# The first expert loop of a MetaFormer block: single chunks through the gate, high halves before low halves, and weight scans issued from another queue

## The reference, cut to what matters

```python
t = _to_tokens(x)                                    # 4096 tokens of 256 values
h = jnp.einsum('nd,ehd->neh', xf, w1)                # xf = layernorm(t); w1, w3: 8 x 512 x 256
g = jnp.einsum('nd,ehd->neh', xf, w3)
eo = jnp.einsum('neh,edh->ned', jax.nn.silu(h) * g, w2)
out = jnp.einsum('ned,ne->nd', eo, comb)             # comb: weights of the two chosen experts
```

## Time and profile before

| | |
|---|---|
| median of 3 runs | 1333.01 us (1328.87 to 1334.24) |
| the profiled execution, its time | 1335.55 us |
| its span, first to last instruction | 1333.8 us |
| PE busy | 945.6 us, 71% |
| DVE busy | 873.4 us, 65% |
| ACT busy | 514.4 us, 39% |
| POOL busy | 442.6 us, 33% |
| mean granted clock of TensorE | 0.811 of full speed |

### The profile page before, as it was taken

How to read it: one execution, slowest core, us unless ns; L and a number is a source line. 1 busy time by engine, 2 the same in 40 slices (tenths; PEclk the granted TensorE clock), 3 DMA queues, 4 the chain that set the end, 5 groups by cost and what they waited for, 6 DMA issues and landing times.

```text
span 1333.8 us, 25140 instructions
## 1 busy us (share of the span) xinstructions
PE 945.6 (71%) x7185; PEld 794.4 (60%) x7185; DVE 873.4 (65%) x1854; ACT 514.4 (39%) x983; POOL 442.6 (33%) x486
## 2 busy tenths in 40 slices
PE   5210577656399999999800668457999999999943
PEld 4100456515288888888700457416888888888842
DVE  6999789897444555555589886683555555555545
ACT  5200223276354444444433443283443333443312
POOL 1285000000045555555522560003444434444410
PEclk8655795558799999999955885557999999999975
DMA  7000007806633555455567312104222232222257
GB/s 229 1 0 0 0 1 224 280 0 201 227 88 94 155 154 155 99 154 158 152 214 241 126 63 77 50 0 103 72 79 71 77 78 75 75 75 75 75 165 252
DMA packets 169438, 147.22 MB, mean 110 GB/s; under 512 B 88432, under 2 KB 152376, under 8 KB 169272
## 3 DMA queue, kind: packets, MB, share of 16 engines
q1 hardware_dynamic: 151048, 103.76, 27.0%
q0 software_dynamic: 14000, 38.82, 9.1%
q10 hardware_dynamic: 4352, 4.20, 1.0%
HBM read 96.39 MB, written 30.93 MB: 95 GB/s over the span
## 4 chain that ended last, share of the span: by engine, by line
PE 57%; DVE 21%; issue 8%; DMA 6%; ACT 5%; SPq 1%; DVEq 1%; ACTq 0%; POOLq 0%; POOL 0%
PE bank L711 27%; PE bank L729 18%; PE bank L647 4%; PE bank L564 3%; DVE tok L1373 2%; DMA wreg<-rows_y 2%; DVE region L1032 2%; PE bank L764 2%; ACT xt L869 2%; DVE xt L1044 2%; DMA wreg<-in_L_ffn_w_dram 1%; PE bank L619 1%; DVE region L1031 1%; DVE region L1343 1%; PE bank L689 1%
## 5 line engine op out<-in xcount | busy, mean ns | idle before, releaser
L711 PE MATMUL bank<-xt,wreg 128*128 x3360 | 382.5, 274 | 30.9 <-DMA xt<-region 30.9
L711 PEld LDWEIGHTS bank<-xt,wreg 128*128 128x128 f16 x3360 | 330.7, 98 | 71.4 <-issue 31.3
L729 PE MATMUL bank<-wreg,region 128*128 128x256 f16 x2520 | 292.6, 273 | 16.2 <-DVE region L1347 15.1
L729 PEld LDWEIGHTS bank<-wreg,region 128*128 128x128 f16 x2520 | 243.6, 98 | 54.0 <-DVE region L1347 24.6
L891 ACT ACTIVATE region<-bank,b_t,fac 128x256 f32<-128x256 f32 x280 | 142.5, 560 | 226.3 <-PE bank L711 215.7
L495 POOL DMA_INDIRECT rows_y<-region,put_now x140 | 138.4, 988 | 221.4 <-DVE region L1358 140.3
L455 POOL DMA_INDIRECT region<-rows_x,fetch_now x144 | 144.4, 1003 | 185.8 <-DMA xt<-region 94.0
L1343 DVE SCALAR_TENSOR_TENSOR region<-bank,fac,region 128x256 f32<-128x256 f32 x140 | 61.2, 479 | 157.8 <-PE bank L711 106.7
L564 PE MATMUL bank<-ident,xn 128*128 128x128 f32 x256 | 56.6, 383 | 112.6 <-DVE xn L1003 104.4
L1350 DVE TENSOR_SCALAR region<-region,fac 128x512 f16<-128x512 f32 x140 | 76.5, 546 | 69.3 <-ACT region L891 64.2
L564 PEld LDWEIGHTS bank<-ident,xn 128*128 128x128 f32 x256 | 45.8, 208 | 121.3 <-DVE xn L1003 110.6
(11 more groups left out here) (237 smaller groups left out, 1238.7 us busy)
## 6 DMA issues: line engine op xcount, KB each, us to landing
wreg<-in_L_ffn_w_dram SPq DMA_DIRECT2D x48, 512.0 KB, 5.9
wreg<-in_L_ffn_w_dram SPq DMA_DIRECT2D x16, 1024.0 KB
wreg<-rows_y SPq DMA_DIRECT2D x48, 256.0 KB, 3.6
region<-in_L_ffn_w_dram SPq DMA_DIRECT2D x12, 1024.0 KB, 7.4
rows_x<-region SPq DMA_DIRECT2D x16, 512.0 KB, 3.2
wreg<-in_x_dram SPq DMA_DIRECT2D x4, 1024.0 KB, 9.4
out_dram<-xt ACTq DMA_DIRECT2D x16, 256.0 KB, 3.6
xt<-region SPq DMA_TRANSPOSE x148
```

What stands on the lines that cost most here:

```text
L711: last = pe.matmul(to, w[:, e, k, ws_, c * P:(c + 1) * P], x_cols[:, bass.ds(b, 1), :, xs_, k, :].rearrange("p j r n -> p (j r) n"), start ...
L729: last = pe.matmul(yb[:, r * C:(r + 1) * C], lhs[:, c, r * P:(r + 1) * P], w[:, e, c, ws_, :], start=first, stop=end, skip_group_check=True)
```

## The change

It has three parts. In `up` of f = 0 PE takes one chunk at a time, `w1` into the left half of a bank and `w3` into the right half, and counts `z_ready` once a chunk; ACT's Silu and DVE's product then go chunk by chunk. In `down` PE does the four matmuls of a chunk that read the high half ahead of the two that read the low half, and for f = 0 it waits for each half apart. The scan loads are issued by ACT: one ahead of the loop, each later one behind an expert's tiles.

```diff
 SP
-            sp.wait_ge(w_lo[0], 6 * E)
-            for e in range(2):
-                load_scan(e)
...
-                    if f == 0 and 1 <= e < E - 1:
-                        sp.wait_ge(scanned, e)
-                        load_scan(e + 1)
 PE, up
-                ws = ((w1_s, zb[2 * (h % 2)]), (w3_s, zb[2 * (h % 2) + 1])) if f == 0 else ((v1_s, zb[h]),)
-                for w, z in ws:
-                    for c in (2 * h, 2 * h + 1):
-                        to = z[:, (c % 2) * TILE:(c % 2 + 1) * TILE]
+                ws = (w1_s, w3_s) if f == 0 else (v1_s,)
+                for c in (2 * h, 2 * h + 1):
+                    for m, w in enumerate(ws):
+                        z, at = (zb[c], m) if f == 0 else (zb[h], c % 2)
+                        to = z[:, at * TILE:(at + 1) * TILE]
...
-                    last.then_inc(z_ready[f], 1)
+                    if f == 0 or c % 2:
+                        last.then_inc(z_ready[f], 1)
 PE, down
-                        pe.wait_ge(lo_ready[0], 2 * halves * tile + c + 1)
+                        pe.wait_ge(hi_ready[0], 2 * halves * tile + c + 1)
...
-                    for r in range(2):
-                        for hs, ws_ in PARTS:
-                            lhs = (hid_hi, hid_lo)[hs]
+                    for hs in range(2):
+                        if f == 0 and hs == 1:
+                            pe.wait_ge(lo_ready[0], 2 * halves * tile + c + 1)
+                        lhs = (hid_hi, hid_lo)[hs]
+                        for r, ws_ in ((0, 0), (0, 1), (1, 0), (1, 1)) if hs == 0 else ((0, 0), (1, 0)):
 ACT
+            def load_scan(n):
+                e = E - 1 - n
+                act.dma_start(scan1[:, n % 2, 0].rearrange("p (c h) -> p c h", c=KC),
+                             v1[e].rearrange("(c p) h -> p c h", p=P)).then_inc(scan_loaded[n % 2], 16)
+                act.dma_start(scan1[:, n % 2, 1].rearrange("p (c d) -> p c d", c=8),
+                             v2[e].rearrange("(c p) d -> p c d", p=P)).then_inc(scan_loaded[n % 2], 16)
...
+                if f == 0:
+                    act.wait_ge(w_lo[0], 6 * E)
+                    load_scan(0)
...
-                                act.wait_ge(z_ready[0], 2 * halves * n + 2 * h + 1)
-                                act.activation(gate_act[:, h], zb[2 * h][:], ACT.Silu, scale=fac[:, 0, e:e + 1]
-                                               ).then_inc(silu_done[f], 1)
+                                for c in (2 * h, 2 * h + 1):
+                                    act.wait_ge(z_ready[0], 2 * halves * n + c + 1)
+                                    act.activation(gate_act[:, h, (c % 2) * TILE:(c % 2 + 1) * TILE], zb[c][:, 0:TILE], ACT.Silu,
+                                                   scale=fac[:, 0, e:e + 1]).then_inc(silu_done[f], 1)
...
+                    if f == 0 and e < E - 1:
+                        free(act, scanned, e)
+                        load_scan(e + 1)
 DVE
-                                dve.wait_ge(z_ready[0], 2 * halves * n + 2 * h + 2)
...
+                                    dve.wait_ge(silu_done[f], 2 * halves * n + c + 1)
+                                    dve.scalar_tensor_tensor(half(hid[:, h], c), zb[c][:, TILE:2 * TILE], fac[:, 1, e:e + 1],
```

More of the change, by code:

```diff
@@ L305, in load_stage1 @@
                              v2[bass.ds(e, 1)].rearrange("a (c p) d -> p (a c) d", p=P)).then_inc(stage_loaded[1][j], 16)
-            def load_scan(n):
-                e = E - 1 - n
-                sp.dma_start(scan1[:, n % 2, 0].rearrange("p (c h) -> p c h", c=KC),
-                             v1[e].rearrange("(c p) h -> p c h", p=P)).then_inc(scan_loaded[n % 2], 16)
-                sp.dma_start(scan1[:, n % 2, 1].rearrange("p (c d) -> p c d", c=8),
-                             v2[e].rearrange("(c p) d -> p c d", p=P)).then_inc(scan_loaded[n % 2], 16)
             def store_rows(f, i):
@@ L1336, in experts @@
                         for h in range(halves):
-                            dve.wait_ge(silu_done[f], halves * n + h + 1)
+                            if f == 1:
+                                dve.wait_ge(silu_done[f], halves * n + h + 1)
                             to_hi, to_lo = (v[:, 2 * h:2 * h + 2].rearrange("p c n -> p (c n)") for v in (hid_hi, hid_lo))
                             if f == 0:
-                                dve.wait_ge(z_ready[0], 2 * halves * n + 2 * h + 2)
                                 half = lambda v, c: v[:, (c % 2) * TILE:(c % 2 + 1) * TILE]
                                 for c in (2 * h, 2 * h + 1):
-                                    dve.scalar_tensor_tensor(half(hid[:, h], c), half(zb[2 * h + 1], c), fac[:, 1, e:e + 1],
+                                    dve.wait_ge(silu_done[f], 2 * halves * n + c + 1)
+                                    dve.scalar_tensor_tensor(half(hid[:, h], c), zb[c][:, TILE:2 * TILE], fac[:, 1, e:e + 1],
                                                              half(gate_act[:, h], c), ALU.mult, ALU.mult).then_inc(hid_ready, 1)
```

## The result

The change made the kernel slower. Its median is 1356.72 us (four runs, 1353.76 to 1364.56); the kernel before, timed beside it, has 1332.53 (four runs). The ratio is 1.0192 with a 95% interval of 1.015 to 1.0234, so 20 to 31 us lost. The profiled execution of the changed kernel is its longest, 1364.56 us. The prediction was 1314 us, 1304 to 1324, with a chance of 0.04 for slower. The rival "Slower than before" (1346 us, transposes that wait for the load) has the right sign and the right wait and is still 11 us short. Its second half, two tiles late at each load, did not come: there is one wait a load.

A forecast was written before the change was run, and what follows sets the result against it. Bound: PE's waits in the first expert loop, 18.0 us for the first transposed columns and 15.1 for DVE's low half. 7.7 + 22.4 - 4.8 - 3.5 - 3.5 + 0.5 = 18.8 us less; forecast 1314 us against 1333.01, range 1304 to 1324.

The forecast's parts named there:

- Slower than before: First expert loop: transposes and the gather behind them wait for each load, making two tiles late; 1346 us, chance 0.04.
- The way in: Entry to the first expert loop: transposes no longer wait behind SP's scan loads, so PE starts 7.7 us earlier.
- loss 3: Seven loads in the loop, issued ahead of the next tile's transposes: 0.5 us each, 3.5 us, bounds 0 and 18.
- this place gets easier, not harder: Tight transpose supply after a load: load 2 us earlier, tile wanted 1.1 us earlier, so more room was claimed.
- The rule: DMA engines alternate between queues packet by packet, so transposes would hardly wait for the load; loss 3 would be 0.
- The tile: First expert loop: a tile falls from 8.51 to 7.85 us, a full gain of 22.4 us over 34 tiles.
- loss 1: Chunk 3's sum seen 0.7 us late by ACT in a fifth of the tiles: 4.8 us, bounds 0 and 20.
- loss 2: DVE's peaks between experts delay the next tile: seven borders of 0.5 us, 3.5 us, bounds 0 and 7.
- the late sum: ACT sees a chunk's sum from PE 0.7 us late, cause unknown; taken off the tile's gain as 4.8 us.
- the peaks: DVE's 4.41 us of work between an expert's last tile and the next; taken off as 3.5 us.
- The Silu of 256 columns: ACT's Silu on one chunk in a tile of the first loop, taken as 0.56 us from the second loop.

The follow-up runs named there:

- e3: The changed kernel with loads 0 and 1 on ACT ahead of the loop, loads 2 to 7 back on SP behind the transposes; 1319.72 us, ratio 0.9904.
- e5: e3 with SP issuing each load in the loop ahead of an expert's last two transposes, not behind them; 1349.18 us, ratio 1.0133.
- e12: The changed kernel with v2 of loads 1 to 5 read in another row order, giving few long packets; ratio 1.026 to the kernel before.

## Why the prediction was wrong, step by step

The account by the repeats: the changed kernel against before is -8.5 us ahead of the loop (means: 368.8 of the thirteen profiles with ACT's entry, 377.3 of the five with SP's), -3.5 in the loop for the compute (278.0 against 281.5), and +37 for seven loads (315 against 278). That is +25; measured were +25.6. (Single profiles of one kernel lie up to 5.7 us apart ahead of the loop, so an agreement to 0.6 us is luck.)

- **The way in**, 7.7 us: right in size and in cause. PE stands still 10.55 instead of 17.96 us, 7.4 less, and what ends last is its sequencer, as worked out. ACT's and SP's order there cost nothing.
- **The load, loss 3**, 3.5 us with bounds 0 and 18: this is the step that failed. "If the transposes wait for the first of the two transfers, they land near 6.5 us into the tile": they landed 12 us into it, together with the end of the second (ACT's queue moves its last packets behind 409 us, the transposes are there at 409.53). I had bounded the worse case by 2.6 us a load. Measured were 5.3 a load, 37 in place of 3.5: 3.9 of waiting (28.5 and 26.1 us in two profiles, seven each) and 1.4 that no term of mine held. The slower matmuls behind a stall (1.6 by the rows) account for those. My argument "before, a tile's gather and transposes together were late by a load of 9 us, and PE never waited" read the wrong pair. Before, 2 MB went out behind one pair of transposes and had over 8 us before the next pair was issued; what ran beside them was a gather. e3's rows show it. The change put them ahead of a pair, and this pair has 2.6 us of room. So "this place gets easier, not harder" was wrong too.
- **The rule** of the Trainium skill, "DMA: Bandwidth & Descriptors", "Queues, rings and completion order" (turns packet by packet), from which I had worked out a loss of 0: the packets of both queues do mix from 402 us on, which agrees with it, but the transposes aren't spared. My working from the rule was at fault: I left out how many packets the transposes have (68 to the load's 82 on an engine, by the estimate above). e5 shows much the same stall with one queue, where no turns between SP and ACT come in.
- **The tile**, 22.4 us less loss 1 and loss 2: mechanism right, size wrong twice. PE's waits for the low half went to nothing, neither the late sum (4.8) nor the peaks (3.5) cost what I took off, and the loop of e3 is 8.17 us a tile with the borders in it (8.15 without them). But 7.85 is not a tile: the gap of 0.37 that the old wait had hidden is exposed (34 x 0.3 = 10 us). And 8.51 was not the usual tile of before: 8.28 was (7.8 us). Measured are 3.5 us.
- **The Silu of 256 columns**: 0.47 us, where I took 0.56. It changed nothing.

Had loss 3 been as small as I put it, the kernel would be e3 or near it: 1320 us, within the range given, but partly by luck: the compute brought 3.5 us of the 14 forecast for it.

## The better kernel

e3 beats both: 1319.72 us (ratio 0.9904, 0.988 to 0.9927), and again 1319.84 us (0.9928, 0.9905 to 0.9951). It keeps the compute of the change and its entry (with load 1 ahead of the loop as well), and leaves the other six loads in the loop where they were. It is 0.7 to 1.0% faster than before.

## What to carry to other kernels

Ask of a bulk transfer not which queue it is on but what small, urgent transfer is issued right behind it: 2 MB ahead of a pair of transposes made them land after 10 us, 1 MB little more than used up their slack, and the same 2 MB behind them cost PE next to nothing, with 0.7 us to spare at the load shown. An idle engine's queue is worth more for this than a busy engine's, since the idle one can wait for the right moment at no cost. Before a term of a sum rests on a short unexplained idle in one profile, take a second profile: here it was 7.8 us of 289 that no other execution had.

## What the runs showed of the hardware

- A transfer of 2.10 MB with two transposes of 0.26 MB behind it, and gather and scatter beside them, kept the 16 DMA engines full for 10 us (share 1.03, 233 GB/s). From the load's first issue the transposes needed 11.8 us on another queue (397.74 to 409.53) and 10.2 on the same one (e5, 432.81 to 443.04).
- The same load behind the transposes slowed the gather beside it: 6.0 us from the gather to the transposes that need it, instead of 2.9 (e3).
- Long packets in the load (e12) made the transposes' wait longer, 5.9 us a load instead of 4.1, and the first load in the loop itself slower, 11.7 us instead of 9.2.
- Behind 11 of 14 stops of PE at a load, of 2.7 to 5.2 us, one tile's 48 `up` matmuls took 6.8 to 8.2 us instead of 5.43; the window behind one of them shows 0.51 of the clock. Behind the other 3 stops they took 5.43.
- One kernel ran its tiles in 8.51 us in one execution and in 8.28 in three others, with the same instructions; in the tiles compared the difference was when ACT saw one sum of PE, 0.7 us later. Its cause stays open, and so does that of the gap of 0.37 us at a tile's start.
